# Attention's operands made ready inside the dense part, its last stores landing during attention, and its first ten products in two bank pairs

## The reference

```python
x = x + 0.5 * ffn(layernorm(x))              # ffn(h) = tanh(h @ W @ A1 @ A2 + bias)
x = x + attention(layernorm(x))
x = x + 0.5 * ffn(layernorm(x))

# attention, per batch and head
content = (q + u_bias) @ k.T
pos = relative_shift((q + v_bias) @ p.T)      # p = pe @ Wp, pe the sinusoidal table
attn = softmax((content + pos) * scale)
out = concat_heads(attn @ v) @ Wo + bo
```

## Time and profile before

| | |
|---|---|
| median of 3 runs | 3433.29 us (3432.21 to 3438.11) |
| the profiled execution | 3432.96 us, of which its span is 3431.2 us |
| granted TensorE clock, mean over the span | 0.988 |
| PE busy | 3357.4 us (98%) |
| ACT busy | 2329.2 us (68%) |
| DVE busy | 1941.3 us (57%) |
| POOL busy | 1326.9 us (39%) |
| moved by DMA | 1231.27 MB, 359 GB/s over the span |

### The profile page before, as it was taken

How to read it: one execution, slowest core, us unless ns; L and a number is a source line. 1 busy time by engine, 2 the same in 40 slices (tenths; PEclk the granted TensorE clock), 3 DMA queues, 4 the chain that set the end, 5 groups by cost and what they waited for, 6 DMA issues and landing times. The chain is left out here.

```text
span 3431.2 us, 110393 instructions
## 1 busy us (share of the span) xinstructions
PE 3357.4 (98%) x34876; PEld 2081.5 (61%) x34876; DVE 1941.3 (57%) x5651; ACT 2329.2 (68%) x3255; POOL 1326.9 (39%) x1341
## 2 busy tenths in 40 slices
PE   8996999999999999999999999999999999999988
PEld 5662566666666666666666666666666666666677
DVE  7771555555555555555555555555555555555557
ACT  3342777777777777777777777777777777777633
POOL 2110444444444444444444444444444444444400
PEclk9996999999999999999999999999999999999999
DMA  5977999999999999999999999999999999999862
GB/s 165 293 246 242 379 390 388 389 390 387 387 387 392 387 388 388 390 388 388 388 389 390 387 387 390 389 387 389 389 389 388 387 388 391 388 388 388 303 197 98
DMA packets 433554, 1231.27 MB, mean 359 GB/s; under 512 B 48993, under 2 KB 133473, under 8 KB 433505
## 3 DMA queue, kind: packets, MB, share of 16 engines
q1 hardware_dynamic: 430000, 1229.12, 95.6%
q10 hardware_dynamic: 3504, 1.53, 0.2%
HBM read 617.04 MB, written 613.43 MB: 359 GB/s over the span
## 5 line engine op out<-in xcount | busy, mean ns | idle before, releaser
L867 POOL TENSOR_SCALAR at_pos_in<-at_pos_in,at_neg_max 128x1024 f32<-128x1024 f32 x1024 | 1145.8, 1119 | 1660.4 <-DVE at_neg_max L830 1660.4
L792 ACT ACTIVATE at_pos_out<-at_ps_pos 128x1024 f32<-128x1024 f32 x1024 | 1049.2, 1025 | 530.8 <-PE at_ps_pos L704 530.8
L830 DVE CUSTOM_DVE_ANT_0 at_pos_in<-at_ps_con,at_pos_in 128x512 f32<-128x512 f32 x1024 | 708.3, 692 | 1188.8 <-PE at_ps_con L704 818.5
L704 PE MATMUL at_ps_con<-at_right,at_left 32*128 32x512 f32 x4096 | 1329.5, 641 | 0.0
L801 ACT ACTIVATE at_prob<-at_ps_turn 128x512 f32<-128x512 f32 x2048 | 1111.5, 595 | 283.1 <-PE at_ps_turn L737 241.8
L704 PE MATMUL at_ps_pos<-at_right,at_left 32*128 32x512 f32 x4096 | 1167.4, 646 | 33.6 <-DMA at_left<-scratch_queries 20.6
L737 PE MATMUL at_ps_turn<-keep_ident,at_pos_in 128*128 128x128 f32 x8192 | 1105.9, 278 | 0.0
L737 PEld LDWEIGHTS at_ps_turn<-keep_ident,at_pos_in 128*128 128x128 f32 x8192 | 890.6, 141 | 156.5 <-issue 154.9
L750 PEld LDWEIGHTS at_ps_pv<-at_prob,at_v_aug 128*32 128x32 f32 x16384 | 385.0, 109 | 773.6 <-issue 773.5
L830 DVE CUSTOM_DVE_ANT_0 at_pos_in<-at_ps_con,at_pos_in,at_neg_half 128x512 f32<-128x512 f32 x1024 | 768.7, 751 | 140.5 <-PE at_ps_con L704 6.1
L750 PE MATMUL at_ps_pv<-at_prob,at_v_aug 128*32 128x128 f32 x16384 | 659.3, 279 | 0.8 <-issue 0.8
(11 more groups left out here) (92 smaller groups left out, 1387.6 us busy)
## 6 DMA issues: line engine op xcount, KB each, us to landing
scratch_scores<-at_pos_out SPq DMA_DIRECT2D x1024, 512.0 KB, 7.3
at_pos_in<-scratch_scores SPq DMA_DIRECT2D x1024, 512.0 KB, 7.5
scratch_queries<-fr_qk SPq DMA_DIRECT2D x128, 256.0 KB, 3.9
at_left<-scratch_queries SPq DMA_DIRECT2D x127, 256.0 KB, 7.3
fr_x<-in_L_attn_x_dram SPq DMA_DIRECT2D x16, 512.0 KB, 7.1
scratch_x<-fr_x_bo SPq DMA_DIRECT2D x16, 512.0 KB, 4.9
scratch_keys<-fr_qk SPq DMA_DIRECT2D x32, 256.0 KB, 5.2
scratch_values<-fr_values SPq DMA_DIRECT2D x8, 1024.0 KB, 5.8
```

Source lines behind the costliest of these rows:

```text
L704: return pe.matmul(banks[:, n, :], left[side][rows, t.i * P:(t.i + 1) * P], right[side][rows, :], start=True, stop=True)
L792: act.activation(pos_out[:, t.slot, :], ps_pos[:, :, :].rearrange("p a m -> p (a m)"), ACT.Copy)\
L830: dve.tensor_tensor_reduce(pos_in[:, t.slot, keys], ps_con[:, n, :], pos_in[:, t.slot, keys], -SCALE, 3.0e38 if n == 0 else neg_half[:, t. ...
L867: pool.tensor_scalar(pos_in[:, t.slot, :], pos_in[:, t.slot, :], -1.0, neg_max[:, t.slot:t.slot + 1], ALU.mult, ALU.add).then_inc(shifted, 1)
```

## The change

- The operands `left`, `right`, `v_in`, `v_aug` and the semaphores of their loads belong to the whole program (`keep`) instead of attention. To make room, `pos` is gone; the position keys pass through `qk[1]`, and ACT waits at g = 2 until they are stored.
- POOL clears the operands at g = 6 and copies the position keys at g = 8; SP issues the first four loads at g = 8. All this stood at the start of attention.
- At the last step ACT issues four of the eight query stores (o = 1), SP the other four.
- SP's list of the dense part ends without a wait. The waits for the stores of x1, queries, keys and values stand in attention now, ahead of the first read.
- The first ten positional products alternate between `ps_pos` and `ps_con`; each waits for the copy of the product two before. PE waits for the tenth copy before the loop.

```diff
-        pos = sb("pos", [P, C, S])
...
-        x_in, x1_out, qk_out, v_out = sems(X_RING, "x_in"), sems(2, "x1_out"), sems(2, "qk_out"), sems(2, "v_out")
+        x_in, x1_out, qk_out, v_out = sems(X_RING, "x_in"), keep["x1_out"], keep["qk_out"], keep["v_out"]
...
+        def store_queries(eng, g, o):
+            k, slot, half = g % 2, g // 2 * H + 1 - o, DH // C
+            for c in range(C):
+                for strip in (2 * o, 2 * o + 1):
+                    eng.dma_start(a["queries"][slot:slot + H, strip, c * half:(c + 1) * half, k * ROWS:(k + 1) * ROWS],
+                                  qk[k][:, o, c, :]).then_inc(qk_out[k], 16)
...
-                        sp.dma_start(a["pos_rows"][:, c * DH // C:(c + 1) * DH // C, :], pos[:, c, :])\
+                        sp.dma_start(a["pos_rows"][:, c * DH // C:(c + 1) * DH // C, :],
+                                     qk[1][:, c, :, :].rearrange("p a m -> p (a m)"))\
...
+                if g == 8:
+                    sp.wait_ge(keep["blanked"], 1)
+                    sp.wait_ge(score_zero, 16)
+                    for k in range(2):
+                        sp.wait_ge(qk_out[k], 16 * QK_STORES)
+                    sp.wait_ge(v_out[0], 16)
+                    query_rows = a["queries"].rearrange("n s d m -> n (s d) m")
+                    sp.dma_start(keep["left"][1][2 * STRIP:P:2, :], query_rows[0, STRIP:2 * STRIP, :])\
+                        .then_inc(keep["first_in"], 16)
+                    sp.dma_start(keep["left"][0][0:P:2, :], query_rows[1]).then_inc(keep["q_in"][0], 16)
+                    sp.dma_start(keep["right"][0][0:2 * STRIP:2, :], a["keys"][0].rearrange("n d m -> (n d) m"))\
+                        .then_inc(keep["k_in"][0], 16)
+                    sp.dma_start(keep["v_in"][0][:, :], a["values"][0, :, :]).then_inc(keep["vals_in"][0], 16)
...
-                    for o, slot in ((0, b * H + 1), (1, b * H)):
-                        for c in range(C):
-                            for strip in (2 * o, 2 * o + 1):
-                                sp.dma_start(a["queries"][slot:slot + H, strip, c * half:(c + 1) * half,
-                                                          k * ROWS:(k + 1) * ROWS], qk[k][:, o, c, :])\
-                                    .then_inc(qk_out[k], 16)
+                    store_queries(sp, g - 1, 0)
+                    if real(g):
+                        store_queries(sp, g - 1, 1)
...
-            sp.wait_ge(score_zero, 16)
-            sp.wait_ge(pos_keys_in, 32)
-            for k in range(2):
-                sp.wait_ge(x1_out[k], 16 * GROUPS // 2)
-                sp.wait_ge(qk_out[k], 16 * QK_STORES * GROUPS // 2)
-                sp.wait_ge(v_out[k], 16 * B // 2)
...
+                    elif g == 2:
+                        act.wait_ge(pos_out, 16 * C)
...
+                    if not real(g):
+                        act.wait_ge(q_copied, g)
+                        store_queries(act, g - 1, 1)
...
-                    act.activation(pos[:, :, :].rearrange("p c m -> p (c m)"),
+                    act.activation(qk[1][:, 0:C, :, :].rearrange("p c a m -> p (c a m)"),
...
+                if g == 6:
+                    for k in range(2):
+                        pool.memset(keep["left"][k][:, :], 0.0)
+                        pool.memset(keep["right"][k][:, :], 0.0)
+                        pool.memset(keep["v_aug"][k][:, :, DH:DH + 1], 1.0)
+                        ins = pool.memset(keep["v_aug"][k][:, :, DH + 1:VW], 0.0)
+                    ins.then_inc(keep["blanked"], 1)
+                if g == 8:
+                    pool.wait_ge(keep["blanked"], 1)
+                    pool.wait_ge(pos_keys_in, 32)
+                    pool.wait_ge(scale2_ready, g + 2)
+                    for k in range(2):
+                        pool.tensor_copy(keep["right"][1 - k][P // 2:P, :],
+                                         keep["pos_keys"][P // 2:P, k * HALF:(k + 1) * HALF]).then_inc(keep["p_ready"], 1)
+                    pool.wait_ge(keep["p_ready"], 2)
...
-            sp.wait_ge(blanked, 1)
-            sp.dma_start(left[1][2 * STRIP:P:2, :], a["queries"][0].rearrange("s d m -> (s d) m")[STRIP:2 * STRIP, :])\
-                .then_inc(first_in, 16)
-            load_queries(Tile(0, 0))
-            load_keys(Tile(0, 0))
-            load_values(Tile(0, 0))
             for w in range(LEAD):
                 write(Tile(0, w))
+                if w == READ_LAG:
+                    for k in range(2):
+                        sp.wait_ge(keep["x1_out"][k], 16 * GROUPS // 2)
+                        sp.wait_ge(keep["qk_out"][k], 16 * QK_STORES * GROUPS // 2)
+                        sp.wait_ge(keep["v_out"][k], 16 * B // 2)
...
-            def positional(t, side):
-                strip(t, side, 2 * STRIP, ps_pos, 0)
-                strip(t, side, 2 * STRIP, ps_pos, 1).then_inc(pos_mm, 1)
-
-            def positional_room(t):
+            def positional(t, side, banks=ps_pos):
+                strip(t, side, 2 * STRIP, banks, 0)
+                strip(t, side, 2 * STRIP, banks, 1).then_inc(pos_mm, 1)
...
-                if t.past(1):
-                    pe.wait_ge(pos_copied, t.count())
+                if t.past(buffers):
+                    pe.wait_ge(pos_copied, t.count(1, 1 - buffers))
...
-            pe.wait_ge(cleared, 1)
             for t in range(LEAD):
-                positional_room(Tile(0, t))
-                positional(Tile(0, t), 1 - Tile(0, t).side)
+                positional_room(Tile(0, t), 2)
+                positional(Tile(0, t), 1 - Tile(0, t).side, (ps_pos, ps_con)[t % 2])
+            pe.wait_ge(pos_copied, LEAD)
...
-            for k in range(2):
-                pool.memset(left[k][:, :], 0.0)
-                ins = pool.memset(right[k][:, :], 0.0)
-            ins.then_inc(blanked, 1)
-            pool.wait_ge(blanked, 1)
-            copy_pos_keys(Tile(0, 0))
-            copy_pos_keys(Tile(0, TILES))
-            for k in range(2):
-                pool.memset(v_aug[k][:, :, DH:DH + 1], 1.0)
-                ins = pool.memset(v_aug[k][:, :, DH + 1:VW], 0.0)
-            ins.then_inc(cleared, 1)
...
+        for name, shape in (("left", [P, S]), ("right", [P, HALF]), ("v_in", [P, P]), ("v_aug", [P, TILES, VW])):
+            keep[name] = [sb(f"{name}{k}", shape) for k in range(2)]
+        keep |= {n: [ctx.enter_context(nc.semaphore(f"keep_{n}{k}")) for k in range(2)]
+                 for n in ("x1_out", "qk_out", "v_out", "q_in", "k_in", "vals_in")}
+        keep |= {n: ctx.enter_context(nc.semaphore("keep_" + n)) for n in ("first_in", "p_ready", "blanked")}
```

20 lines of the change are left out of this document (9 added, 11 removed).

## The result

| | before | changed |
|---|---|---|
| median of 4 runs, us | 3433.32 (3432.21 to 3438.11) | 3411.18 (3409.86 to 3411.66) |
| ratio, 95% interval | | 0.9932 (0.9915 to 0.9949) |
| profiled execution / its span, us | 3432.96 / 3431.2 | 3411.35 / 3409.6 |
| mean granted clock | 0.988 | 0.991 |

The changed kernel is 0.68% faster, 22.1 us by the medians and 21.6 us by the spans; 3410 was forecast. The total is right, but two of its three terms were sized too high and the third too low. First the page: busy time, PE's busy tenths in 40 slices, and the time to landing of a write.

The account below looks back on a forecast made before the run. PE's program was taken to pace attention, with a few us of DMA room, so an earlier start moves the end equally. 9.5 + 13.7 + 0 + 0 = 23.2 us; 3432.96 - 23.2 + 0.33 = 3410 us, range 3405.5 to 3418.

Parts of the forecast that it names:

- Part 1: Seam before attention: wait for landing, clearing and loads leave the path, PE starts at 297.9 instead of 307.44; 9.5 us.
- rival (d): End of dense part: barrier still holds PE until the stores have landed; 2.7 us less, 3413; 0.09 together with (c).
- (c): First dozen tiles: DMA holds them back, or PE's clock falls again; 4.5 us less, 3414.5; 0.09 together with rival (d).
- the bytes are the same, ACT only lets them begin earlier: Last stores at the seam: ACT's first at 286.7 instead of SP's at 288.10, so the drain ends 1.4 us earlier.
- Rival (b): Seam: SP's issue, not the drain, set the 0.925 us; 2.3 to 5 us more, 3405 to 3408; chance 0.08.
- Part 2: Ten first positional products in two bank pairs: 15.3 us instead of 29.0, so 13.7 us won.
- rival (a): Ten products: the clock stays at half throughout; 7.1 us won there, 16.6 in all, 3416.7; chance 0.25.
- I take 6 us: Ten products: the clock rises 6 us after PE's start, three products at half clock, then seven at full.
- Part 3: First nine tiles of attention: 27.6 us as before, 0 us net, from 3 us better to 4.5 us worse.
- the 2 us for the reads: First tiles: scores read back through DRAM at 17.3 us, content product ready at 15.3; DVE waits some 2 us once.
- Part 4: Dense part: moved clearing, position copies and loads fit into idle time and cost nothing; 2 us allowed.
- Rival (e): Steady attention: DMA, not PE, paces all 1024 tiles where landing passes 11.4 us; costs 29 us, 3440; chance 0.03.

Follow-up runs that it names:

- the two experiments: Changed kernel with SP's wait for the stores put back: seam 15.39 us; kernel before with only the two bank pairs added: seam 20.50 us.
- without the split: Changed kernel, but SP issues all eight last query stores and ACT none; ratio to the kernel before 0.9955, seam 12.64 us.
- the values last and the bridge: Changed kernel, last values stored after last keys and queries, 7 spare 128-row products ending PE's dense list; ratio 0.9936, ten products 12.24 us.
- full-height among: Changed kernel with one spare 128-row product behind each of the first four tiles' products; one run, ten products 27.79 us.
- strip bridge: Changed kernel with 22 spare 32-row products at the end of PE's dense list; one run, seam 12.18 us, ten products 18.55 us.
- the shorter one: Changed kernel, last values stored after last keys and queries, 14 spare 32-row products ending PE's dense list; one run, ten products 18.23 us.

## Why the prediction was right, and where it was not

**Part 1, the seam: forecast 9.5 us, measured 7.85.** The mechanism was right: the wait for landing, the clearing and the loads left the path (2.3 to 2.8 and 5.1 us, by the two experiments), PE starts one barrier behind SP's last issue, and the change does what it says (rival (d) is out: the stores' transfers ran until about 302, and PE had started at 300.61; (c) is out too: no transfer held back the first tiles). Wrong is the 1.4 us for ACT's head start. The step "the bytes are the same, ACT only lets them begin earlier" took the drain for a fixed amount at a fixed rate. The rate fell instead, from 306 GB/s over 289 to 301 to 282 over 289 to 300, at the same share of 1.00, and SP ended where it had; without the split it was 305 again. Why two issuers move less stays open. The lower end of the bounds, nothing gained by ACT, 8.1 us, was the measured case. Rival (b) is out too. The Trainium skill, "DMA: Bandwidth & Descriptors", section "Issuing engines are not separate DMA queues", was cited for a second issuer saving only issue time; the runs agree with its direction (12.64 us without the split, 12.78 with it) and show that here even that much was not saved.

**Part 2, the ten products: forecast 13.7 us, measured 10.43.** Two errors that partly cancel. The clock did not rise: rival (a)'s mechanism is what happened. The step that failed is "I take 6 us": it took two rises, both in stretches in which full-height work or four strips at once ran, for evidence on products that use two strips. 17.4 us without a pause were not enough. And the price of the half clock was mis-sized, both in the forecast and in rival (a): 2.08 us is the duration of one tile's four records standing alone, while the pitch of tiles back to back is (316.10 - 302.45) / 8 = 1.71 us, since the end of one overlaps the beginning of the next. 18.55 us were measured where (a) had 21.9, so rival (a), with the right mechanism, would have missed the total by more (16.6 us against 21.6). The Trainium skill, "TensorE: Matmul & The Clock Gate", section "What's actually happening", calls the warm-up a budget of time; the trace doesn't bear this out for these products, 17.4 us of which left the clock at half.

**Part 3, the first tiles: forecast 0 us, measured 3.68.** Two terms were wrong, a count and a wait. The step "nine tiles in 27.6 us, against 9 x 2.84 = 25.6" counted one tile too many: 27.6 us are eight tiles, against 8 x 2.84 = 22.7. The kernel before lost 4.9 us there and not 2, in waits for copies (1.04, 1.11 and 0.60 us in PE's timeline behind 336.42) and at half clock. By the prediction's own terms eight tiles would then have come to 22.7 + 2 = 24.7, 2.9 us better; measured were 23.94. The second term is the 2 us for the reads. They were not late, because PE ran its ten products at 1.71 us and not at 1.15. DVE's first total waited for PE:

```profile
321.41 0.69 DVE L857 CUSTOM_DVE_ANT_0 at_pos_in<-at_ps_con,at_pos_in 128x512 f32<-128x512 f32 x1 [32.33 <-PE at_ps_con L731]
```

The mechanism itself is real: in the run with the values last and the bridge, where the products did come every 1.11 us, DVE waited for the first read and PE for DVE, 3.88 us against the 2 forecast. So parts 2 and 3 are coupled: of what faster products win, the reads take a part back. SP's moved waits cost nothing, as forecast: SP waited only for ACT up to 330 us. Over parts 2 and 3 together, where the cut between them doesn't matter, 13.7 us were forecast and 14.1 measured. That is luck: the clock won nothing, a product cost less than was taken, and the tiles before had been miscounted.

**Part 4, the dense part: forecast 0, measured 0**, against a scatter of 2.3 us in its end.

**Rival (e)** did not happen where the change was measured, though the landing rose there, from 7.5 to 10.2 us. Its threshold of 11.4 us was about right: on the chips where a write lands after 11.4 us or more, attention is 30 to 60 us longer, the size it was priced at (29 us) or twice that. But the cause given, writes that begin in a full queue, isn't needed: the kernel before shows the same there, and gets into it slowly, 1000 us behind the seam.

The total was near because the errors had opposite signs: -1.65, -3.3 and +3.7, and -0.4 us from the stretches that the edit doesn't touch.

## What to carry to other kernels

Before giving stores to a second issuer, look at what the first one is held by: a key store held SP 0.8 us ahead of the 1 MB store and of ACT's stores, 1.2 to 1.6 us behind the large one, and 2.8 us behind both, and putting the large one last was worth 6.2 us. Count tiles by their instructions before multiplying by a pitch. Price a run of equal instructions by the distance of their starts, not by the duration of one that stands alone. When a producer that is read back through DRAM gets faster, add up producer and read-back as one chain, since what the one wins the other may wait.

## What was not expected of the hardware

- The granted clock stayed at half through 17.4 us of products without a pause, each on two of four strips of 32 rows; where it was up when they began, it stayed up for 12 us of the same products. It rose 10.4 us (changed kernel) and 14.6 us (full-height among) behind the first content product, from which on four strips are in use at once; in the kernel before, with pauses between, 15.7 us. The first transposes had come 1.4, 5.6 and 4.2 us before the rise. What the chip looks at stays open.
- Products on two strips also held a clock that was up for the 9.7 us of the strip bridge, and let it fall 1.1 us after the end of the shorter one (6.28 us), 0.4 us into attention.
- Four store issues by a second engine lengthened the first one's: 5.50 us for two key stores against 3.21 without them, and the whole moved 282 GB/s instead of 305, at a DMA share of 1.00 and 1.01.
- One program ran 1.4% longer on four chips than in the first measurement: there 381 GB/s flow instead of 388, and the landing of a write creeps up over some 1000 us until SP waits for it.
